# Dissolving the context block of a twelve-layer decoder: its squares, roots and part of its transposes into the self-attention ahead, the rest into the slot attention behind

## What is computed

```
sn = rmsnorm(slots) * slot_norm_w;  ctx_n = rmsnorm(context) * input_norm_w
a  = softmax over slots of (sn Wq)(ctx_n Wk)^T / sqrt(128), then divided by its sum over the context (+1e-6)
slots = gru_cell(a @ ctx_n Wv, slots)
```

## Time and profile before

| | us |
|---|---|
| median of three runs | 1163.63 |
| the profiled execution, its own time | 1168.05 |
| its span, first to last instruction | 1166.3 |
| busy: PE, DVE, ACT, POOL | 914.9, 756.6, 570.1, 255.2 |
| mean granted clock of PE | 0.85 |

### The profile page before, as it was taken

The page is one execution under the profiler, slowest core; times in us unless marked ns, Lnnn a source line. Parts: engine busy times, 40 slices in busy tenths (PEclk is TensorE's granted clock), DMA queues, the critical chain, the costliest instruction groups (busy, mean ns, idle before and its releaser), DMA issues. The chain is left out here.

```text
span 1166.3 us, 18306 instructions
## 1 busy us (share of the span) xinstructions
PE 914.9 (78%) x6163; PEld 567.9 (49%) x6163; DVE 756.6 (65%) x2181; ACT 570.1 (49%) x1660; POOL 255.2 (22%) x349
## 2 busy tenths in 40 slices
PE   5985599999878465168866879885786999999986
PEld 2344499999746222133544358554582233333323
DVE  6457667777658289364577745632647888888823
ACT  3236367777541311032353533452252677777773
POOL 4006245555400022021302000134400111111100
PEclk8698699999979678565986779798695899999997
DMA  9500000000000620100001000553022011111000
GB/s 236 144 1 1 0 2 2 1 2 2 1 1 1 84 29 0 28 1 1 2 1 32 19 1 1 149 133 90 15 45 64 1 25 26 26 26 20 2 1 15
DMA packets 76177, 35.83 MB, mean 31 GB/s; under 512 B 35226, under 2 KB 74562, under 8 KB 76083
## 3 DMA queue, kind: packets, MB, share of 16 engines
q1 hardware_dynamic: 73714, 33.61, 13.2%
q0 software_dynamic: 896, 0.63, 0.2%
q10 hardware_dynamic: 1472, 0.41, 0.2%
HBM read 24.42 MB, written 11.05 MB: 30 GB/s over the span
## 5 line engine op out<-in xcount | busy, mean ns | idle before, releaser
L527 ACT ACTIVATE L3x_E<-L3x_pS 128x400 f32<-128x400 f32 (+1 forms) x384 | 167.8, 507 | 48.9 <-PE L3x_pS L621 48.0
L443 DVE TENSOR_REDUCE L3x_NMP<-L3x_pM 128x1 f32<-128x361 f32 x384 | 178.1, 525 | 19.0 <-PE L3x_pM L599 18.0
L599 PE MATMUL L3x_pM<-ctx_tm 64*128 64x361 bf16 x384 | 104.4, 341 | 14.0 <-DVE L3x_NMP L443 9.9
L621 PE MATMUL L3x_pS<-ctx_tm 64*128 64x400 bf16 (+1 forms) x384 | 107.6, 350 | 3.4 <-ACT L3x_E L527 2.1
L1473 ACT ACTIVATE L0x_E<-L0x_E,ctx_r 128x100 f32<-128x100 f32 x288 | 105.1, 369 | 9.6 <-DVE L0x_E L1380 9.6
L636 PE MATMUL L3x_pO<-L3x_E,CT 128*32 128x400 f32 (+1 forms) x768 | 85.5, 517 | 0.0
L599 PEld LDWEIGHTS L3x_pM<-ctx_tm 64*128 64x128 bf16 x384 | 30.4, 96 | 110.4 <-DVE L3x_NMP L443 91.1
L1562 PE MATMUL L0x_pU<-ctx_tm,L0x_E 128*100 128x129 f32 x576 | 70.5, 279 | 2.9 <-POOL L0x_E L1293 2.9
L1552 PE MATMUL L0x_pS<-L0x_QS,CT 128*128 128x100 f32 x576 | 70.8, 281 | 0.0
L1562 PEld LDWEIGHTS L0x_pU<-ctx_tm,L0x_E 128*100 128x100 f32 x576 | 67.2, 171 | 4.5 <-POOL L0x_E L1293 4.0
L1293 POOL TENSOR_TENSOR L0x_E<-L0x_E,L0x_RZ 128x1200 f32<-128x1200 f32 x24 | 52.7, 2194 | 75.0 <-DVE L0x_RZ L1400 75.0
(11 more groups left out here) (631 smaller groups left out, 2126.7 us busy)
## 6 DMA issues: line engine op xcount, KB each, us to landing
ctx_tm<-in_ctx SPq DMA_DIRECT2D x8, 704.0 KB
ctx_tm<-key_terms SPq DMA_DIRECT2D x16, 270.8 KB, 4.4
key_terms<-ctx_tm SPq DMA_DIRECT2D x42, 90.2 KB
ctx_tm<-in_L_ffn_wi SPq DMA_DIRECT2D x4, 512.0 KB, 8.1
ctx_tm<-in_L_ffn_wo SPq DMA_DIRECT2D x4, 512.0 KB
ctx_tm<-query_terms SPq DMA_DIRECT2D x16, 75.0 KB, 3.7
...
```

Of the source, the lines that this page charges most:

```text
L443: nc.vector.tensor_reduce(NMP[:, p, i // NC4, a, i % NC4:i % NC4 + 1], v, AX.X, ALU.max, negate=True).then_inc(s_mr, 1)
L527: nc.scalar.activation(E[0:r, n % EB, :], pS[0:r, n % 3, 0:NG * T], ACT.Exp, scale=SCALE8).then_inc(s_e, 1)
L599: nc.tensor.matmul(pM[:, n % 3, 0:CW], key_rows(QS, a)[:, b, p, 128 * x:128 * x + 128], key_rows(KS, a)[:, b % KB, c, p, :], start=True, s ...
L621: nc.tensor.matmul(pS[0:NW[k], n % 3, 0:NG * T], key_rows(KS, a)[:, b % KB, k % 4, p, 128 * (k // 4):128 * (k // 4) + NW[k]], key_rows(QS, ...
```

## The change

The context block is gone. Its work goes to two places.

**Into the self-attention (only where `beside` is set):** all 96 squares go to ACT: 24 ahead of tick 0, then four behind the exps of an even unit and five behind the exps and `outT` of an odd one. The scale 1/128 is inside the Square, the sums lie in one tile of 128x96. Behind the last maximum, in ticks 17 to 25, PE turns one group a tick (`late_context`, the nine groups of batches 5, 6, 7), in the two PSUM banks of the max scores; DVE copies the first five, ACT the last four. PE also forms the query product (tick 19), turns the GRU weights (21) and multiplies them (23), with DVE's copies in the same ticks; DVE adds 1e-6 (tick 21), ACT loads the table of Sqrt and takes the roots (its tick 21), DVE does two reciprocals, two fused steps and the products of column 129 (`context_roots`, tick 24). POOL forms the gate bias when the last exps is done, each step behind a wait for the one before. `KN` now lies in `m.XNT` and `V` in `m.XN2`, since the last third of `m.CT` is being filled; ACT's copies into `KN` wait until PE has formed the values, which read `m.XNT`.

**Into the slot attention:** the 15 groups of batches 0 to 4 are turned in the first part of the block, between the first steps of the pipeline, whose order on each engine is written out; the letters of `COPIED_BY` say whether ACT (A) or DVE (V) copies. `sums(0)` stands behind `less_max(1)` on DVE; `update(0)` waits for the last group ACT copies. Ticks begin at 0.

The diff, cut to its core (eight spaces of indentation are left out; the new weights' buffers, the DVE steps `query_weights` and `gate_weights`, which are as before on new buffers, and `query_product` are left out too; `ALU`, `s_...` semaphores as in the text):

```diff
...
-QN, KN = spare[:, at:at + TOK], spare[:, at + TOK:at + 2 * TOK]
...
+    V = spare[0:T, at:at + B * VH * 32].rearrange("p (b h d) -> p b h d", b=B, h=VH)
+else:
+    KN = m.XNT
+    V = m.XN2[:, :, :].rearrange("t b (h d) -> t b h d", h=VH)
...
+LATE, BY_VECTOR = 9, 5
+SQ_EVEN, SQ_ODD, TURN_LAST = 4, 5, N + 1
+SQ_FIRST = B * NKT - (SQ_EVEN + SQ_ODD) * B
...
             pool.wait_ge(q.norm, B)
             beside[1](nc, pool, m, s_table)
+            chain = Chain(pool, s_gb)
+            bi, bh = gw["x0bi"], gw["x0bh"]
+            pool.wait_ge(m.loaded["L0x"], m.load_total["L0x"])
+            pool.wait_ge(s_e, N)
+            nc.gpsimd.tensor_tensor(grow[0:1, 0:2 * D], bi[0:1, 0:2 * D], bh[0:1, 0:2 * D], ALU.add)
+            nc.gpsimd.tensor_copy(grow[0:1, 2 * D:3 * D], bi[0:1, 2 * D:3 * D])
+            nc.gpsimd.tensor_copy(grow[0:1, 3 * D:4 * D], bh[0:1, 2 * D:3 * D])
+            nc.gpsimd.memset(m.gate_parts[:, :], 0.0)
+            chain.then(nc.gpsimd.memset(m.gate_ones[:, :], 1.0))
+            for row in (0, 32, 64):
+                chain.then(nc.gpsimd.tensor_copy(part[0:1, :], grow[0:1, :]))
+                chain.then(nc.gpsimd.tensor_copy(m.gate_parts[row:row + 1, :], part[0:1, :]))
+                if row < 64:
+                    chain.then(nc.gpsimd.tensor_tensor(grow[0:1, :], grow[0:1, :], part[0:1, :],
+                                                       ALU.subtract))
         if causal:
             for u in range(N):
...
+        def late_context(i):
+            dve.wait_ge(s_ct, i + 1)
+            nc.vector.tensor_copy(m.CT[:, B - 3 + i // 3, i % 3 * 512:(i % 3 + 1) * 512], pM[:, i % 2, :])\
+              .then_inc(s_cv, 1)
...
+        def gru_copies():
+            for i, out in enumerate((m.wihT, m.whhT)):
+                dve.wait_ge(s_wt, i + 1)
+                nc.vector.tensor_copy(out[:, :], pS[:, i, 0:3 * D]).then_inc(s_wc, 1)
+        def gate_weights():
+            dve.wait_ge(s_w3, 1)
+            nc.vector.tensor_scalar(m.gate_w[:, :], pX[:, 0:3 * D], gw["x0iw"][:, 0:1], None, ALU.mult)
+        def mean_squares():
+            dve.wait_ge(s_sq, B)
+            nc.vector.tensor_scalar(ss[:, :, :], ss[:, :, :], 1e-6, None, ALU.add).then_inc(s_ms, 1)
+        def context_roots():
+            chain.then(nc.vector.reciprocal(m.ctx_r[:, :, :], ss[:, :, :]))
+            dve.wait_ge(s_rt, 1)
+            nc.vector.reciprocal(rc[:, :, :], rt[:, :, :])
+            chain.then(nc.vector.scalar_tensor_tensor(out=m.ctx_r[:, :, :], in0=rt[:, :, :], scalar=0.5,
+                                                      in1=m.ctx_r[:, :, :], op0=ALU.mult, op1=ALU.mult))
+            chain.then(nc.vector.scalar_tensor_tensor(out=m.ctx_r[:, :, :], in0=rc[:, :, :], scalar=0.5,
+                                                      in1=m.ctx_r[:, :, :], op0=ALU.mult, op1=ALU.add))
+            nc.vector.tensor_tensor(m.ctx_tm[:, :, 0:KT_FULL, D], ss[:, :, 0:KT_FULL],
+                                    m.ctx_r[:, :, 0:KT_FULL], ALU.mult)
+            nc.vector.tensor_tensor(m.ctx_tm[0:TAIL, :, KT_FULL, D], ss[0:TAIL, :, KT_FULL],
+                                    m.ctx_r[0:TAIL, :, KT_FULL], ALU.mult)
         for i in range(NQ):
             query(0, i)
...
+                if 0 <= t - TURN_LAST < BY_VECTOR:
+                    late_context(t - TURN_LAST)
+                if t == N + 3:
+                    query_weights()
+                if t == N + 5:
+                    gru_copies()
+                    mean_squares()
+                if t == N + 7:
+                    gate_weights()
+                if t == N + 8:
+                    context_roots()
         stats(B - 1)
...
+        def squares(lo, hi):
+            for i in range(lo, min(hi, B * NKT)):
+                b, k = divmod(i, NKT)
+                if k == 0:
+                    act.wait_ge(m.ctx_loaded[b], 32)
+                    if b >= 1:
+                        act.wait_ge(s_sq, b)
+                ins = nc.scalar.activation(junk[:, k, :], m.ctx_tm[:, b, k, 0:D], ACT.Square,
+                                           scale=float(D) ** -0.5, accum_out=ss[:, b, k:k + 1])
+                if k == NKT - 1:
+                    ins.then_inc(s_sq, 1)
+        def late_context(i):
+            act.wait_ge(s_ct, i + 1)
+            nc.scalar.copy(m.CT[:, B - 3 + i // 3, i % 3 * 512:(i % 3 + 1) * 512], pM[:, i % 2, :])\
+              .then_inc(s_ca, 1)
...
+        def context_roots():
+            act.wait_ge(s_ms, 1)
+            nc.scalar.activation(rt[:, :, :], ss[:, :, :], ACT.Sqrt).then_inc(s_rt, 1)
...
+            squares(0, SQ_FIRST)
...
+            if beside is not None and 0 <= t - S_AT < N:
+                u = t - S_AT
+                lo = SQ_FIRST + (SQ_EVEN + SQ_ODD) * (u // 2) + SQ_EVEN * (u % 2)
+                squares(lo, lo + (SQ_ODD if u % 2 else SQ_EVEN))
+            if beside is not None:
+                if BY_VECTOR <= t - TURN_LAST < LATE:
+                    late_context(t - TURN_LAST)
+                if t == N + S_AT:
+                    load_table(nc, m, ACT.Sqrt)
+                    context_roots()
...
+        def late_context(i):
+            if i == 0:
+                pe.wait_ge(s_mr, N)
+            if i % 3 == 0:
+                pe.wait_ge(m.ctx_loaded[B - 3 + i // 3], 32)
+            if 2 <= i < BY_VECTOR + 2:
+                pe.wait_ge(s_cv, i - 1)
+            elif i >= 2:
+                pe.wait_ge(s_ca, i - 1 - BY_VECTOR)
+            for k in range(4):
+                last = nc.tensor.transpose(pM[:, i % 2, k * 128:(k + 1) * 128],
+                                           m.ctx_tm[:, B - 3 + i // 3, 4 * (i % 3) + k, 0:D], m.ident[:, :])
+            last.then_inc(s_ct, 1)
...
+        def gru_turned():
+            pe.wait_ge(s_e, N)
+            for i, key in enumerate(("x0ih", "x0hh")):
+                for c in range(3):
+                    last = nc.tensor.transpose(pS[:, i, c * D:(c + 1) * D], gw[key][:, c, :], m.ident[:, :])
+                last.then_inc(s_wt, 1)
+        def gate_product():
+            pe.wait_ge(s_wr, 1)
+            pe.wait_ge(s_wc, 1)
+            nc.tensor.matmul(pX[:, 0:3 * D], gw["x0v"][:, :], m.wihT[:, :], start=True, stop=True)\
+              .then_inc(s_w3, 1)
...
                     weigh(b)
+            if beside is not None:
+                if 0 <= t - TURN_LAST < LATE:
+                    late_context(t - TURN_LAST)
+                if t == N + 3:
+                    query_product()
+                if t == N + 5:
+                    gru_turned()
+                if t == N + 7:
+                    gate_product()
...
-def context_block(nc, m, name, stats):
...
-    TICKS = range(-4, N + 1)
+    TICKS = range(N + 1)
     SB = 5
     QT, UT_AT = 256, 256
     G4 = 512
+    EARLY = 15
+    COPIED_BY = "AAAVAVAVAVAVAVA"
...
+turn_banks = [[pS[:, 3, :], pS[:, 4, :], pU, pG][i % 4] if i < 6 else [pU, pG][i % 2] for i in range(EARLY)]
...
+        for n in range(4):
+            rstd(n)
+        normalise(0)
...
-        ln_vector(nc, dve, chain, m, q)
-        dve.wait_ge(m.loaded[name], m.load_total[name])
-        dve.wait_ge(s_w2, 1)
-        nc.vector.tensor_scalar(Mqk[:, :], pS[:, 4, 0:D], w["x0sw"][:, 0:1], float(D) ** -0.5,
-                                ALU.mult, ALU.mult).then_inc(s_wr, 1)
...
+        def context(i):
+            dve.wait_ge(s_ct, i + 1)
+            nc.vector.tensor_copy(m.CT[:, i // 3, i % 3 * 512:(i % 3 + 1) * 512], turn_banks[i][:, :])\
+              .then_inc(s_cv, 1)
...
+        first_slots(0)
+        slot_stats(0)
+        first_slots(1)
+        first_slots(2)
+        slot_norm(0)
+        for b in (3, 4, 5):
+            first_slots(b)
+        context(3)
+        slot_stats(1)
+        first_slots(6)
+        first_slots(7)
+        slot_norm(1)
+        less_max(0)
+        slot_stats(2)
+        context(5)
+        slot_norm(2)
+        slot_stats(3)
+        context(7)
+        less_max(1)
+        sums(0)
+        slot_norm(3)
+        for i in (9, 11, 13):
+            context(i)
...
-            if i == -3:
-                gru_copies()
...
-            if i == -2:
-                gate_bias()
-                gate_weights()
...
+        def context(i):
+            act.wait_ge(s_ct, i + 1)
+            nc.scalar.copy(m.CT[:, i // 3, i % 3 * 512:(i % 3 + 1) * 512], turn_banks[i][:, :])\
+              .then_inc(s_ca, 1)
+        ln_root(nc, act, m, q, 1)
+        context(0)
+        context(1)
+        slotsT(0)
+        context(2)
+        queries(0)
+        load_table(nc, m, ACT.Exp)
+        context(4)
+        exps(0, 0)
+        slotsT(1)
+        context(6)
+        exps(0, 1)
+        queries(1)
+        exps(0, 2)
+        slotsT(2)
+        context(8)
+        queries(2)
+        for i in (10, 12, 14):
+            context(i)
         for i in TICKS:
             if 0 <= i + 1 < N:
                 exps(i + 1, 0)
...
+        def context(i):
```

(35 more changed lines are left out.)

184 lines of the change are left out of this document (47 added, 137 removed).

## The result

Four runs of each kernel on one chip: 1163.41 us before (1161.76 to 1164.21), 1134.25 us after (1132.60 to 1134.68). The ratio is 0.9751, with a 95% interval from 0.9725 to 0.9778: 29.2 us faster. The forecast was 1137.4 us, in 1130 to 1149.

A forecast was written before the change was run, and what follows sets the result against it. No engine was taken as full: the kernel is a chain of blocks that all engines enter together. -28.5 + 7.3 - 5.0 = -26.2 from the median 1163.63 gave 1137.4 us, range 1130 to 1149.

The forecast's parts named there:

- The block removed: Between self-attention and slot attention: the context block's 28.9 us go, less a 0.4 us block change; -28.5 us.
- The tail: End of the self-attention: inserted groups, products, roots and context_roots make the block end at 98.0; +7.3 us.
- The price of a group: Self-attention's end, on PE: four transposes take 0.6 us, and each group pushes what follows.
- the roots' wait: Ticks 21 and 22: ACT's roots, ahead of outT(6), wait for DVE's copies; with PE's insertions, projection 4.4 us late.
- Squares: Self-attention, on ACT: 96 squares, 0.3 us apart, hidden in ACT's wait for PE; cost 0.
- POOL: Self-attention's end: the gate bias chain takes 9.9 to 15.5 us and ends at 97, just hidden by 98.0.
- The filling: Slot attention's start: update(1) at 29.1 us into the block, third update at 36.7 against 42.3; -5.0 us with the clock.
- the clock's term: Slot attention's filling: one short half-clock stretch at the start, when PE waits for others anyway; priced -0.6 us.
- filling at half clock: Rival, 13%: PE's gaps keep the slot attention's filling at half clock, so 8.1 us of gain are gone; 1145 us.
- From the second update on nothing changes: Slot attention from its second update on, and all behind: no change, so the gain is counted up to the third update.
- the tail hides it: Rival, 8%: PE's and DVE's insertions fall into their waits, tail +3.0, filling gives 2 more; 1131 us.
- Square is not in Exp's table: Rival, 5%: ACT loads a table twice for each of 16 self-attention units; net +6, 1169 us.

The follow-up runs named there:

- mean_early: Changed kernel with mean_squares issued on VectorE behind the sixth sequence's residual instead of behind the two GRU copies; 1136.28 us.
- no_late: Changed kernel without the nine late context groups and their copies, the last three sequences' turned context set to zeros; 1132.57 us (one execution).
- sums_first: Changed kernel with sums(0) issued on VectorE ahead of less_max(1) instead of behind it; 1135.91 us.
- turns_back: Changed kernel with all 24 groups of context transposes put back into a block of their own between self-attention and slot attention; 1150.20 us.
- busy_tail: Changed kernel with sixteen idle transposes added behind the last projection of the self-attention; 1136.26 us (one execution).

## Why the forecast was right

Up to the third update the forecast was -26.2 us and the traces show -26.8, or -26.5 counted from the last maxima copy. The mechanism was the one that was forecast, but that the sum came out so close is luck: the tail was forecast 1.9 us too dear and the filling 1.6 too cheap.

**The block removed (-28.5).** From the block's first transposes (91.19 in the earlier trace rows) to the slot attention's first step (119.63 in the earlier trace rows) were 28.4, and all of it went. Right.

**The tail (+7.3; measured +5.4, from the maxima copy to the end of the stretch).** The end was named rightly: `context_roots` and not PE stood ahead of the last residual, 2.2 us for the 2.4 priced, and 1.87 of them came back when it moved. (The 6 ns for each number of a reciprocal do not follow from the row of 64 in 0.55 us alone, but 0.72 and 0.75 us came for the 0.75 forecast.) Too dear was what stood ahead of it: the score 1.6 us late instead of 2.3 to 2.8, the projection 3.3 instead of 4.4, the last turn 3.3 instead of 4.8. Two steps failed there. The price of a group was misread: 0.6 us is 48 transposes in 7.10 us, but for 3.4 of those 7.1 us the clock was half. The kernel before, its windows:

```profile
92.30:95.70 3.40, 3.40 (x18) 3.40 (x17) 3.40 (x24) 3.01 (x17) 1.57 (x1) 0.50 0.01 2
```

In the changed kernel's tail the clock was full, and PE's next step started 0.53, 0.59 and 0.44 us behind the three groups and 0.31 behind the product (priced 0.5): 1.87 instead of 2.3. The steps just ahead of the groups handed over 0.07 to 0.09 sooner each, so 1.6 remain. That PE "has hardly a gap where the group stands" was right. And the roots' wait was charged on top of PE's insertions, when the two lay beside each other: mean_early took the wait away and gained 0.35, no_late took the groups away and left PE waiting 0.87 for the roots.

*Squares* at cost 0 held: 304 ns each, no load of a table, and 0.22 us at most at the last exps.

*POOL* was to end at 97, just hidden; it ended at 91.4, after 8.2 us where 9.9 to 15.5 were forecast. Its copies of 512 were 0.60 us and its tensor-tensor 1.15, below the low bounds of 0.7 and 1.5. The same steps on VectorE in the kernel before took 0.39 (cast), 0.28 (copy) and 0.68 us. The Trainium skill ("GPSIMD Engine Reference", Engine selection) puts two-input work at about twice VectorE's time and one-input work near line rate; by these rows two inputs cost 1.7 times VectorE's time and one input 1.5 to 2.1 times, on one partition, so the trace does not bear out the second. The low end of the range, to which that page had pointed, was the better one all the same.

**The filling (-5.0; measured -3.4).** Its mechanism held step by step: scaled query ready 5.1 us behind the first step, as forecast, `update(0)` released by ScalarE's last copy and not by the product, as sums_first confirmed, then updates 7.3 apart. The step that was mis-sized is the clock's term. "One short stretch at half at the start, when PE waits for others anyway: -0.6" were two stretches in the changed kernel. A short one does cost next to nothing (mean_early), but the first here lasted 6.8 us and cost 0.9, and the second took in `scores(1)`: 5.44 us for 2.92, on the path, because groups 8 to 14, the last copy and `exps(1)` all queue behind them. At full clock the filling is 35.5 us, 1.2 less than the 36.7 forecast; at the clock that the kernel got, 38.8. Since one profile without this stretch (sums_first) has the same instructions up to there, which clock the kernel would get was hardly to be had from the rows of the kernel before.

The rival *filling at half clock*, at 13%, was thus right in one of its scores and in the early groups; its price for a score (2.3 us) is near the 2.5 measured for the one, and the updates, which it had at half clock, ran at full. The Trainium skill ("TensorE: Matmul & The Clock Gate", PE-mode transpose), which says that transposes do not bring the full clock, is not borne out: in turns_back the clock was 0.50 from 93.7 to 97.0 and 1.00 from 97.1 to 105.9, while PE did nothing but transposes, as the earlier trace rows had let one expect.

**Behind.** "From the second update on nothing changes": in instructions, yes. The medians differ by 29.2 us, so 2.4 more than the distance up to the third update, and most of what the time came out below the forecast of 1137.4 is this. The profiled pair differs by 6.9 there. The traces show where 2.6 us of it are, in the stage of the tiles named `L1a`, which starts 242 us behind the third update. VectorE's and GpSimd's timelines, of the kernel before and then of the changed one:

```profile
465.56 3.22 DVE L1981 TENSOR_TENSOR L1a_O<-L1a_OA,L1a_L 128x80 f32<-128x80 f32 x2
...
465.52 2.88 POOL L1920 TENSOR_TENSOR L1a_W<-CT,L1a_KV 128x1280 f32<-128x1280 f32 x1 [4.03 <-ACT CT L2031]
```

```profile
439.75 0.53 DVE L2090 TENSOR_TENSOR L1a_O<-L1a_OA,L1a_L 128x80 f32<-128x80 f32 x2
...
440.38 4.19 POOL L2029 TENSOR_TENSOR L1a_W<-CT,L1a_KV 128x1280 f32<-128x1280 f32 x1 [4.70 <-ACT CT L2140]
```

Two small products on VectorE, issued just behind the start of a long one on GpSimd, took as long as that one; otherwise they take 0.53 us. It is so in both profiles of before (3.22 and 3.17 us), in turns_back, sums_first and busy_tail (3.18, 3.11, 3.12), and in none of the nine others. From the first VectorE step on a tile of `L1a` to the first on one of `L1x`, those five took 95.0 to 96.4 us, the nine others 93.1 to 94.1. The last three of the five have the changed kernel's instructions there, so the change does not remove this coincidence; it comes by the moment at which GpSimd starts. Whether this alone makes the 2.4 us of the medians is not shown. The rest of the difference is scatter: the same program took 997.5, 999.8 and 1006.6 us behind the third update.

The rival *the tail hides it* was wrong in its mechanism though near in time: the tail's insertions showed, and the filling did not give more. *Square is not in Exp's table* was wrong.
